# Reordering the split output weights of an attention kernel, and moving the softmax scaling of its first six units from ScalarE to VectorE

## The reference, cut to what matters

```python
x = x + attention(xn, w_qkv, w_o) + ffn(xn, W, b, A, B, gate_w, gate_b)
# attention: 32 heads, 8 key/value heads, D = 128, causal
scores = q @ k.T / sqrt(D) - slope[head] * sqrt(distance)   # -inf above the diagonal
attn   = softmax(scores);  out = attn @ v;  result = out @ w_o
# ffn: xn @ W.T + b, plus one low-rank product per token chosen by a gate
```

## Time and profile before

| | us |
|---|---|
| median of 3 runs | 2504.72 (2502.26 to 2505.23) |
| the profiled execution, own time | 2503.76 |
| its span | 2502.0 |
| PE busy in the span | 2413.1 (96%) |
| DVE busy | 1506.7 (60%) |
| ACT busy | 1385.0 (55%) |
| POOL busy | 780.6 (31%) |

### The profile page before, as it was taken

The page is one execution under the profiler, slowest core; times in us unless marked ns, Lnnn a source line. Parts: engine busy times, 40 slices in busy tenths (PEclk is TensorE's granted clock), DMA queues, the critical chain, the costliest instruction groups (busy, mean ns, idle before and its releaser), DMA issues.

```text
span 2502.0 us, 35041 instructions
## 1 busy us (share of the span) xinstructions
PE 2413.1 (96%) x12128; PEld 2051.0 (82%) x12128; DVE 1506.7 (60%) x2817; ACT 1385.0 (55%) x3075; POOL 780.6 (31%) x1029
## 2 busy tenths in 40 slices
PE   5999999997899999999799999999999999999999
PEld 4787888886778888888788888888888888888887
DVE  6657455565655555555566666666666676666665
ACT  4532133334533223333777777778777677777764
POOL 3211000000320000000343645546345464454644
PEclk9999999999999999999999999999999999999999
DMA  4536344546344544544755565655656556555543
GB/s 149 189 127 217 138 153 167 202 168 219 111 147 173 189 144 175 203 152 156 269 185 185 188 221 180 220 187 186 215 198 208 182 195 216 192 204 203 185 169 127
DMA packets 118320, 455.95 MB, mean 182 GB/s; under 512 B 11945, under 2 KB 12089, under 8 KB 109184
## 3 DMA queue, kind: packets, MB, share of 16 engines
q1 hardware_dynamic: 86176, 334.37, 38.7%
q0 software_dynamic: 31968, 119.33, 13.7%
HBM read 276.96 MB, written 176.69 MB: 181 GB/s over the span
## 4 chain that ended last, share of the span: by engine, by line
PE 90%; DVE 5%; ACT 2%; issue 1%; DMA 1%; POOL 1%; DVEq 0%; SPq 0%; ACTq 0%; POOLq 0%
PE ps L656 28%; PE ps L658 28%; PE ps L657 28%; PE ps L843 5%; DVE stats L1151 1%; ACT rows L934 1%; DVE pt_lo L1137 0%; DVE w_lo L1137 0%; DVE probs L1374 0%; ACT res_hi L905 0%; DMA lora_lo<-lora_s 0%; DVE wo L1137 0%; DVE res_a L1227 0%; PE ps L738 0%; DVE res_b L1137 0%
## 5 line engine op out<-in xcount | busy, mean ns | idle before, releaser
L905 ACT ACTIVATE w_hi<-raw 128x1024 fp32r<-128x1024 f32 x196 | 207.0, 1059 | 560.0 <-PE ps L658 440.0
L1137 DVE TENSOR_TENSOR w_lo<-raw,w_hi 128x1024 fp32r<-128x1024 f32 x196 | 239.2, 1224 | 358.0 <-ACT w_hi L905 357.7
L1405 DVE TENSOR_TENSOR acc<-ps,acc 128x512 f32<-128x512 f32 x448 | 298.2, 687 | 235.2 <-issue 210.8
L656 PE MATMUL ps<-x_hi,w_hi 128*128 128x512 f32 x1120 | 436.5, 390 | 0.0
L657 PE MATMUL ps<-x_lo,w_hi 128*128 128x512 f32 x1120 | 435.9, 389 | 0.0
L658 PE MATMUL ps<-x_hi,w_lo 128*128 128x512 f32 x1120 | 435.8, 389 | 0.0
L1045 ACT ACTIVATE probs<-probs,neg_max 128x512 f32<-128x512 f32 (+3 forms) x512 | 284.1, 567 | 176.5 <-DVE neg_max L1374 176.4
L656 PE MATMUL ps<-wo,op_hi 128*128 128x512 f32 x896 | 362.5, 405 | 18.4 <-DVE wo L1137 18.4
L658 PE MATMUL ps<-wo,op_lo 128*128 128x512 f32 x896 | 353.6, 395 | 0.0
L657 PE MATMUL ps<-wo,op_hi 128*128 128x512 f32 x896 | 352.2, 393 | 0.0
L1374 DVE CUSTOM_DVE_ANT_0 probs<-ps,bias 128x512 f32<-128x512 f32 (+3 forms) x512 | 220.5, 486 | 96.9 <-PE ps L658 93.4
(11 more groups left out here) (158 smaller groups left out, 4780.3 us busy)
## 6 DMA issues: line engine op xcount, KB each, us to landing
raw<-w_all SPq DMA_DIRECT2D x70, 1024.0 KB, 5.2
q<-qk_s SPq DMA_DIRECT2D x128, 512.0 KB, 3.9
acc<-acc_s SPq DMA_DIRECT2D x128, 512.0 KB, 5.2
acc_s<-acc SPq DMA_DIRECT2D x112, 512.0 KB, 7.8
qk_s<-res_hi POOLq DMA_DIRECT2D x40, 1024.0 KB, 4.6
qk_s<-res_a POOLq DMA_DIRECT2D x20, 1024.0 KB, 9.1
qk_s<-res_b POOLq DMA_DIRECT2D x20, 1024.0 KB, 5.2
k<-qk_s SPq DMA_DIRECT2D x32, 512.0 KB, 3.6
```

The costliest lines, as they stand in the source:

```text
L656: pe.matmul(to, st_hi, mv_hi, start=start, stop=False, skip_group_check=True)
L905: nc.scalar.activation(to, source, ACT.Copy).then_inc(signal, 1)
L1137: nc.vector.tensor_tensor(to, source, high.bitcast(F32), ALU.subtract).then_inc(signal, 1)
L1405: nc.vector.tensor_tensor(to, fill[f % 2][:, :], to, ALU.add).then_inc(s_acc, 1)
```

## The change

Two edits. The tables of the w_o steps are rewritten: in place 8 POOL makes sum 5 right after sums 2 and 3 (it was in place 9), and ACT and DVE take step 6 there, last in the iteration (it was in place 10); in place 9 step 2 is made last by DVE (it was early in place 10) and step 3 early in place 10 (it was last in place 9), and ACT's two highs are 2, 3 instead of 3, 2. LOWS_MIDDLE goes. The second edit: in units 0 to 5 DVE multiplies the probabilities by row_inv, in place, directly after the reciprocal, and ACT doesn't.

```diff
+EARLY = 6
-WO_SUMS_IN = {6: (4,), 8: (2, 3), 9: (5,)}
-WO_ORDER = (0, 1, 4, 3, 2, 6, 5)
-HIGHS_FIRST = {9: (4,), 10: (6,)}
-HIGHS_LAST = {6: (0,), 7: (1,), 9: (3, 2), 10: (5,)}
-LOWS_EARLY = {9: (4,), 10: (2,)}
-LOWS_MIDDLE = {10: (6,)}
-LOWS_LAST = {6: (0,), 7: (1,), 9: (3,), 10: (5,)}
+WO_SUMS_IN = {6: (4,), 8: (2, 3, 5)}
+WO_ORDER = (0, 1, 6, 4, 2, 3, 5)
+HIGHS_FIRST = {9: (4,)}
+HIGHS_LAST = {6: (0,), 7: (1,), 8: (6,), 9: (2, 3), 10: (5,)}
+LOWS_EARLY = {9: (4,), 10: (3,)}
+LOWS_LAST = {6: (0,), 7: (1,), 8: (6,), 9: (2,), 10: (5,)}
@@ ACT
-                if n < UNITS:
+                if EARLY <= n < UNITS:
                     normalise(n)
@@ DVE, inverses(n)
                 nc.vector.reciprocal(row_inv[:, :], row_sum[:, :]).then_inc(s_inv, 1)
+                if n < EARLY:
+                    dve.wait_ge(s_inv, n + 1)
+                    for i in range(QT):
+                        tile = probs[:, n % 2, OFF[i]:OFF[i] + (i + 1) * P]
+                        last = nc.vector.tensor_scalar(tile, tile, row_inv[:, i:i + 1], None, ALU.mult)
+                    last.then_inc(s_probs, 1)
@@ DVE, the loop
-                for f in todo[1:3]:
-                    add_fill(*f)
-                for part in making(n, LOWS_MIDDLE):
-                    out_split(*part)
-                for f in todo[3:]:
+                for f in todo[1:]:
                     add_fill(*f)
```

## The result

The changed kernel takes 2507.8 us (median of 22 runs, 2504.42 to 2511.08); the kernel before, measured again beside it, 2503.39 (22 runs). The ratio is 1.0016 with a 95% interval of 1.0011 to 1.0022: 4.0 us slower (2.8 to 5.5; the two medians lie 4.4 apart), inside the 0.2% within which I had called it no change, but clear of zero over so many runs. The forecast was 2506, range 2490 to 2517.

The account below looks back on a forecast made before the run. PE, busy in 96% of the span, was taken as the bound. Profiled 2503.76 plus 4.9 (boundaries) minus 3.2 (first units) gave 2505.5; with 0.96 up to the runs' median 2506.4, rounded to 2506, range 2490 to 2517.

Parts of the forecast that it names:

- The wait for the low of 2 goes: At each group boundary PE's 2.2 us wait for step 2's low disappears, as that low is made at iteration 21's end.
- Sum 5 on POOL ends at 1409.5, after two overlaps of 1.0 us: In POOL's queue, behind sum 3, stretched by DVE's lows of steps 6 and 4; bounds 1407.5 and 1409.5.
- ACT is 4.2 us late: ACT's op_hi of the third part starts at 1411.1 instead of 1406.90, and everything behind it moves by that.
- The boundary costs 4.3 us: Each of seven group boundaries: 4.1 us of waiting plus 0.2 for the clock, 30.1 in all instead of 25.2.
- It is a wait for pt_lo, about 4 us together with those for op_lo and the third transposes: PE's boundary cost of 4.1 us: attend waits for pt_lo, with smaller waits for op_lo and at_raw inside it.
- The clock's fall is covered: Slow TensorE clock at a boundary falls mostly into PE's waiting time; 0.2 us a boundary, bounds 0 and 1.6.
- Rival (c): TensorE runs two fills at 1.2 GHz, so a boundary costs 5.7 us or more; 2516 in all; chance 0.15.
- (b): Milder collisions on POOL: sum 5 ends near 1408.0, a boundary costs 2.8 us; 2496 in all; chance 0.20.
- The first units gain 3.2 us: First six units and group 0's boundary: iteration 7 starts 3.2 us earlier; bounds 0.8 and 4.65.
- Rival (d): DVE's scaling collides with POOL in units 2 and 5, leaving 0.8 of the 3.2 us gain; 2509; chance 0.10.
- Rival (a): ACT does not wait for POOL and the group boundaries cost nothing; 2475 in all; chance 0.12.

Follow-up runs that it names:

- a quarter of sum 5: The changed kernel with three of the four pieces of POOL's sum for step 5 left out, all orders and waits kept; ratio 0.9958 to the kernel before.

## Why the prediction came out right, step by step

- *The wait for the low of 2 goes.* Right: no such wait is left.
- *Sum 5 on POOL ends at 1409.5, after two overlaps of 1.0 us.* Right: in the changed kernel it ends at 1406.70, 0.81 us after iteration 22 begins; the predicted point was 0.83 after it. Both overlaps are there (3.84 and 3.82 instead of 2.8).
- *ACT is 4.2 us late.* It waits 4.15. The experiments make this the cause and not a companion: over six kernels the iteration follows ACT's wait, nearly one for one (it takes 0.1 to 0.5 us more).
- *The boundary costs 4.3 us.* It costs 4.6, so 7.1 us more than before instead of 4.9. The term that was too small is the low of step 2: I moved the low that stood there before it, of step 3, as it was (the first row), and the new one takes 1.80. It starts 0.01 us after the start of POOL's out_sum of the second tile (the second row), 0.02 after it with step 6 back (1.80 again), and 0.01 with a quarter of sum 5 (1.83). That is 0.4 us a boundary, 2.8 us over seven. The sum lacks 2.2, because the 0.2 a boundary for the clock was not needed; 4.1 and 0.4 leave 0.1 a boundary that is not accounted for. (1415.60 + 4.2 + 0.2 is 1420.0, too, and not 1419.9.)

```profile
1410.42 1.40 DVE L1137 TENSOR_TENSOR wo<-wo_sum,wo 128x1024 fp32r<-128x1024 f32 x1 [1.81 <-ACT wo L905]
```

```profile
1411.87 0.73 POOL L611 TENSOR_TENSOR op_raw<-at_raw,at_raw 128x256 f32<-128x256 f32 x1
```

- *It is a wait for pt_lo, about 4 us together with those for op_lo and the third transposes.* Only in part. The profile gives PE 2.0 us for op_lo and 0.4 for the add of the first fill, and none for the third transposes: the slow clock filled that time. Without it (the tables alone, fourth boundary) the waits are 1.95, 0.90 for at_raw and 0.91 for the add, 3.8 together. The prediction had the two fills after the transposes end 0.7 us before pt_lo; it did not count that the third fill waits for the add, which stands directly before pt_lo on DVE. So the third fill ends together with pt_lo. The size came out all the same, since both stand behind the same maxima.
- *The clock's fall is covered.* It fell in all seven boundaries, during the first fill and the transposes, as I had put it there, and cost nothing that can be seen: in the kernel with the tables alone boundaries with the fall and without it are equally long. Rival (c), 5.7 us a boundary, did not come about, and neither did (b), in which sum 5 ended early.
- *The first units gain 3.2 us.* 2.86 in the profile. The parts are right as well: the scaling takes 1.27 us alone (1.4 taken), about 3.2 beside POOL (up to 4.4 allowed), and all the gain lies in iteration 6. How the two edits share it is open. In iteration 6 the tables alone bring 2.99 us and the scaling alone 0.46. Up to the start of iteration 7 it is 1.6 and 1.1, differences as large as those between profiles of kernels that should be alike there.
- *Rival (d), the scaling collides with POOL.* It did, in units 2 and 5 (and in 1), where the rule of the Trainium skill that I had cited for it (SBUF — State Buffer, Who interferes with whom) said it would if a tensor_scalar runs in its two-port mode; the trace agrees, 3.23 and 3.02 us against 1.27, but does not show the mode. But the gain did not shrink to 0.8: the low of 2 behind the scaling of unit 5 ended at 1251.67 + 1.75 = 1253.42, and the third fill of iteration 6, which wants it, starts at 1255.82, held for 0.2 us by the add and not by the low.
- *Rival (a), the boundaries cost nothing*, is nearly what the order of steps 2 and 3 brings once POOL doesn't stand in between: in the kernel with sum 5 on DVE and step 6 back a boundary costs 0.3 us, and the whole is 24 us faster than before.

The sum of the prediction was +1.7 us and the measured difference is +4.0. The mechanism was right, but a part of the closeness is luck. The forecast in absolute terms (2506) is only 1.8 below the measured 2507.8, because the three runs it started from had a median 1.3 above that of the 22.

## What to carry to other kernels

When work is moved to an earlier place in an in-order queue, what counts is who waits for the entries that now stand behind it, and what those in turn hold up: here 3.8 us of POOL, whose result nobody wanted for another 5 us, stopped ACT and through it PE. Before such a move, look for the margin at the end of that chain (here 1415.60 against 1415.82, none), and for an engine that is already waiting at that spot: the same sum on DVE, where it waited for ACT, made the edit worth 0.7%, and 1% with step 6 back in its old place. And undo edits one by one: of the four in this change, one is the gain (step 2 before step 3), two ate it, and one, the scaling, was worth nothing that can be measured. Of the two that ate it the early sum 5 could not simply be left out, because the low of 2 waits for all four sums; what was free was the engine that makes it.

## What was not expected of the hardware

- Four short instructions lose more beside POOL than one long one. Four scalings of 128 to 512 columns take 1.27 us alone and 3.23 beside POOL's pieces of 0.7 us, about half a microsecond of waiting for each, while a single low of 1.22 us beside POOL's pieces takes 1.4 to 1.8. Whether the number of instructions makes the difference or their kind was not varied. POOL's side is the other way round: the low costs it 1.0 us, and the four scalings hardly anything (sums 2 and 3 of group 0 take 2.88 and 3.96 us instead of 2.81 and 3.80).
- The profile puts PE's wait for POOL's op_lo down to "issue" (13.9 us, 7 times). Its end, 1409.93, lies 0.1 us after the first op_lo piece ends (1409.11 + 0.7), and it shrinks with POOL's work in the experiments; so a wait called "issue" on PE can be one for another engine.
